# Softmax preparation moved into the second recurrent step and the second graph layer, layernorms placed afresh

## What is computed

```python
# L0: y = (adj @ x + x) @ weight + bias, each row divided by its length
# L1: 5 recurrent steps, in_matrix and out_matrix both adj
m = adj @ h
z = sigmoid([m, m] @ w3.T + b3 + h @ u3.T + ub3)
r = sigmoid([m, m] @ w4.T + b4 + h @ u3.T + ub3)
hv = tanh([m, m] @ w5.T + b5 + (r * h) @ u5.T + ub5)
h = (1 - z) * h + z * hv
# L2: A = adj + I, d = rowsum(A) ** -0.5
y = (d[:, None] * A * d[None, :]) @ x @ W.T + b
# L3: the k-th positive cell of adj gets e[k], cells that aren't positive get -9e15
A = softmax(where(adj > 0, e[cumsum(adj > 0) - 1], -9e15), axis=1)
y = (A * I) @ (x @ W[0]) + (A * (1 - I)) @ (x @ W[1]) + bias
```

## Time and profile before

| | us |
|---|---|
| median of 3 runs (lowest, highest) | 800.88 (800.42, 801.36) |
| the profiled execution's own time | 799.98 |
| its span, first to last instruction | 798.3 |
| PE busy | 770.0 (96%) |
| DVE busy | 651.3 (82%) |
| ACT busy | 515.2 (65%) |
| POOL busy | 117.1 (15%) |
| mean granted PE clock | 0.993 |

### The profile page before, as it was taken

The page is one execution under the profiler, slowest core; times in us unless marked ns, Lnnn a source line. Parts: engine busy times, 40 slices in busy tenths (PEclk is TensorE's granted clock), DMA queues, the critical chain, the costliest instruction groups (busy, mean ns, idle before and its releaser), DMA issues.

```text
span 798.3 us, 12062 instructions
## 1 busy us (share of the span) xinstructions
PE 770.0 (96%) x3822; PEld 638.7 (80%) x3824; DVE 651.3 (82%) x1578; ACT 515.2 (65%) x1050; POOL 117.1 (15%) x127
## 2 busy tenths in 40 slices
PE   7999988899999999999999999999999999999996
PEld 6888766687888888888888888888877787888885
DVE  6788999988877777777778777777999999986444
ACT  4768756678666666666666666666677766665445
POOL 1354422200000000000000000000112133332222
PEclk9999999999999999999999999999999999999998
DMA  6300000100100000000000000000000000000112
GB/s 186 128 1 2 1 0 1 53 1 9 45 1 0 1 1 0 0 0 0 0 0 0 0 0 0 0 1 1 1 1 1 1 2 1 1 0 14 53 54 93
DMA packets 8782, 13.09 MB, mean 16 GB/s; under 512 B 2336, under 2 KB 3872, under 8 KB 8480
## 3 DMA queue, kind: packets, MB, share of 16 engines
q1 hardware_dynamic: 8736, 12.53, 4.6%
HBM read 7.28 MB, written 5.24 MB: 16 GB/s over the span
## 4 chain that ended last, share of the span: by engine, by line
PE 67%; DVE 24%; ACT 5%; issue 2%; DMA 1%; SPq 0%; POOL 0%; ACTq 0%
PE agg_ps L930 11%; PE agg_ps L932 11%; PE agg_ps L931 11%; PE gate_ps L860 5%; PE gate_ps L862 5%; PE gate_ps L861 5%; PE cand_ps L860 3%; PE cand_ps L862 3%; DVE stats L765 3%; PE cand_ps L861 3%; PE turn_ps L969 3%; PE gate_ps L867 3%; PE cand_ps L867 3%; DVE nat_lo L777 2%; DVE cand L733 2%
## 5 line engine op out<-in xcount | busy, mean ns | idle before, releaser
L576 POOL TENSOR_TENSOR rstd<-mean_var,half 128x4 f32<-128x4 f32 x64 | 78.5, 1226 | 570.6 <-DVE mean_var L772 570.5
L930 PE MATMUL agg_ps<-adj_hi,nat_hi 128*128 128x512 f32 x384 | 151.9, 396 | 0.0
L932 PE MATMUL agg_ps<-adj_hi,nat_lo 128*128 128x512 f32 x384 | 150.1, 391 | 0.0
L931 PE MATMUL agg_ps<-adj_lo,nat_hi 128*128 128x512 f32 x384 | 149.6, 390 | 0.0
L462 ACT ACTIVATE reset_hi<-gate_r 128x512 fp32r<-128x512 f32 x80 | 50.6, 632 | 105.2 <-DVE gate_r L741 105.2
L724 DVE TENSOR_TENSOR agg_lo<-agg_ps,agg_hi 128x512 fp32r<-128x512 f32 x80 | 55.1, 689 | 63.6 <-ACT agg_hi L429 63.5
L390 ACT ACTIVATE res<-res,shift,rstd 128x128 f32<-128x128 f32 x210 | 87.9, 484 | 10.1 <-DVE shift L784 10.1
L932 PEld LDWEIGHTS agg_ps<-adj_hi,nat_lo 128*128 128x128 f32 x384 | 72.0, 188 | 16.1
L931 PEld LDWEIGHTS agg_ps<-adj_lo,nat_hi 128*128 128x128 f32 x384 | 72.2, 188 | 15.6
L930 PEld LDWEIGHTS agg_ps<-adj_hi,nat_hi 128*128 128x128 f32 x384 | 72.2, 188 | 15.0
L446 ACT ACTIVATE gate_r<-gate_ps,bias 128x512 f32<-128x512 f32 x80 | 55.1, 689 | 39.4 <-PE gate_ps L862 39.4
(11 more groups left out here) (174 smaller groups left out, 1705.6 us busy)
## 6 DMA issues: line engine op xcount, KB each, us to landing
res<-in_x SPq DMA_DIRECT2D x16, 256.0 KB, 5.5
out<-res SPq DMA_DIRECT2D x16, 256.0 KB, 2.0
rows<-in_adj SPq DMA_DIRECT2D x4, 256.0 KB, 3.9
mix_rows<-feat SPq DMA_DIRECT2D x1, 1024.0 KB, 3.9
later<-mix_rows SPq DMA_DIRECT2D x1, 1024.0 KB, 4.8
gate_z<-in_L_gnn_w_w SPq DMA_DIRECT2D x3, 128.0 KB, 5.4
gate_r<-in_L_gnn_bias SPq DMA_DIRECT2D x2, 64.0 KB, 5.5
gate_z<-in_L_gnn_u_w SPq DMA_DIRECT2D x2, 64.0 KB, 4.6
```

What stands on the lines that cost most here:

```text
L576: pool.tensor_tensor(rstd[:, i % RING, :], mean_var[:, i % RING, :, 1], half[:, :], ALU.pow).then_inc(rstd_made, 1)
L930: pe.matmul(ps, nat_hi[:, b, k, :], m_hi[:, k, :], start=(k == 0), stop=False)
L931: pe.matmul(ps, nat_hi[:, b, k, :], m_lo[:, k, :], start=False, stop=False)
L932: last = pe.matmul(ps, nat_lo[:, b, k, :], m_hi[:, k, :], start=False, stop=(k == T - 1))
```

## The change

The L0 layernorm moves up: added in slot n+4, measured in n+4, normed in n+6, split and turned in n+7, copied in n+8. Results of the fifth step are turned 4 to 10 slots after their unit, five in about seven slots; the transposes of L2 ("cross") come six slots later than before, in slots 107 to 122. Except in L0 and for the last unit, ACT norms all four quarters. Epsilon, the sign and the shift go from DVE to POOL, which has four operations a unit for its one. "chosen" and "value" go to slots 24 to 35, one every three slots; "late" comes in slots 26 to 35; exponentials to slots 99 to 102, scaling (now ACT, two a slot) to 104 and 105, diagonal to 105, "mix" turns to 106 to 109. `mix` and `chosen` now lie over eye_hi and eye_lo, `count` and `mask` over `later`. The raw scores, not the weights, go through DRAM. The L2 matrix no longer comes from POOL's sums: the adjacency is loaded a second time after slot 35, ACT scales its rows in slots 38 and 39, PE turns it in slots 41 to 44 and adds the diagonal by a small matmul. The loop covers two steps; step two is written out. W_L3 and W_SELF are loaded after the mix is stored. A Sigmoid stands at ACT's start.

```diff
-LOOP_FROM = 2 * B
-LOOPS = STEPS - 2
+LOOP_FROM = 3 * B
+LOOPS = STEPS - 3
...
-LAGS = {"turn": (0, 0), "add": (1, 1), "stats": (6, 1), "shift": (7, 2), "norm": (11, 3), "split": (12, 4),
-        "back": (13, 5)}
-RING = 16
-SLOTS = UNITS + 1 + LAGS["norm"][1] + 1
+LAGS = {"turn": (0, 0, 0, 0), "add": (2, 1, 1, 1), "stats": (2, 1, 1, 1), "norm": (4, 3, 3, 3), "split": (5, 4, 4, None),
+        "cross": (5, None, 10, None), "back": (6, None, 11, None)}
+RING = 8
+SLOTS = UNITS + 1 + LAGS["norm"][3] + 1
...
+    if is_inner(u):
+        return STATE_LAG
+    return 2 if stage(u) == L0 else STATE_LAG + (u - LAST) * 2 // 5 if is_step(u) else 1
+
+
+def lag(what, u):
+
+    if what == "add" and B - 2 <= u < B:
+        return 1
+    return LAGS[what][0 if stage(u) == L0 else 1 if is_step(u) else stage(u) - L2 + 2]
...
-    return [u for u in NORMED if u + turn_lag(u) + LAGS[what][stage(u) != L0] == s]
+    return [u for u in NORMED if lag(what, u) is not None and u + turn_lag(u) + lag(what, u) == s]
 
 
 def shared(n):
 
-    return stage(n) == L0 or n == UNITS - 1 or len(norms_at(n + turn_lag(n) + LAGS["norm"][1], "norm")) == 2
+    return stage(n) == L0 or n == UNITS - 1
...
 OWNER_AT = 3
-CHOSEN_AT = 5
-VALUE_AT = 9
+SUM_AT = 3
 WEIGHTS_AT = 13
-D_ROW_AT = B + 3
-
-SUM_AT = 3
-LATE_AT = 4
-EXP_AT = VALUE_AT + 1
-EYE_AT = B
-L2_ROWS_AT = D_ROW_AT + 1
-MIX_MADE_AT = B + 4
-L2_AT = L2_ROWS_AT + 6
-MIX_AT = AFTER + 9
-DIAGONAL_AT = AFTER + 4
+
+CHOSEN_AT = [B + 8 + 3 * k for k in range(T)]
+LATE_AT = [at + 2 for at in CHOSEN_AT]
+VALUE_AT = [at + 2 for at in CHOSEN_AT]
+SCALE_AT = VALUE_AT[-1] + 3
+L2_AT = SCALE_AT + 3
+assert L2_AT + T < LOOP_FROM
+
+EXP_AT = AFTER + 3
+INV_AT = EXP_AT + T
+WEIGH_AT = INV_AT + 1
+DIAGONAL_AT = INV_AT + 2
...
     if MIX_AT <= s < MIX_AT + T:
         found.append(("mix", s - MIX_AT))
-    found += [("back", u) for u in norms_at(s, "split") if stage(u) in (L0, L2)]
+    found += [("back", u) for u in norms_at(s, "cross")]
...
-    if VALUE_AT <= s < VALUE_AT + T:
-        found.append(("value", s - VALUE_AT))
-    if s == D_ROW_AT:
-        found.append(("d_row", 0))
+    if s in CHOSEN_AT:
+        found.append(("chosen", CHOSEN_AT.index(s)))
+    if s in VALUE_AT:
+        found.append(("value", VALUE_AT.index(s)))
+    if L2_AT <= s < L2_AT + T:
+        found.append(("l2", s - L2_AT))
...
         adj_lo = sb("adj_lo", [P, T, N], F32R)
+        with nc.sbuf_tensor("mix", [P, T, N], F32) as mix:
+            pass
         eye_hi = sb("eye_hi", [P, T, N], F32R)
+        with nc.sbuf_tensor("chosen", [P, T, N], F32) as chosen:
+            pass
         eye_lo = sb("eye_lo", [P, T, N], F32R)
         later = sb("later", [P, T, N])
...
-            sp.dma_start(mix_dram.rearrange("(p t) m -> p t m", t=T), mix).then_inc(mix_stored, 16)
+            sp.wait_ge(late_added, T)
+            sp.dma_start(later[:, :, :], adj.rearrange("(p t) m -> p t m", t=T)).then_inc(rows_again, 16)
+            sp.wait_ge(max_made, T)
+            sp.dma_start(mix_dram.rearrange("(p t) m -> p t m", t=T), mix[:, :, :]).then_inc(mix_stored, 16)
+            sp.dma_start(w_all[:, W_SELF, :], wl3[0]).then_inc(last_in, 16)
+            sp.dma_start(w_all[:, W_L3, :], wl3[1]).then_inc(last_in, 16)
             sp.wait_ge(mix_stored, 16)
-            sp.wait_ge(l2_lo_made, T)
+            sp.wait_ge(turn_read, reads(TURN_NO["l2", T - 1]))
             sp.dma_start(later[:, :, :], mix_dram.rearrange("(p t) m -> p t m", t=T)).then_inc(mix_loaded, 16)
             sp.dma_start(diag[:, :], mix_dram.rearrange("n m -> (n m)")[0:N * N:N + 1]
                          .rearrange("(p t) -> p t", t=T), allow_slow_non_contiguous=True).then_inc(diag_in, 16)
...
                         act.wait_ge(turned, k + 1)
-                        if n in (4, 6, 8, 10, 12):
-                            act.wait_ge(turned, TURN_NO["chosen", T - 1] + 1)
-                        if n == 6:
-                            act.wait_ge(late_added, T)
-                        if n == 8:
-                            act.wait_ge(turned, TURN_NO["value", T - 1] + 1)
-                        if n == 10:
-                            act.wait_ge(l2_made, T)
-                        if n == 12:
...
                         act.wait_ge(gate_done, n + 1)
                         for t in range(T):
-                            if n or t:
-                                act.wait_ge(squared, T * n + t)
-                            act.activation(square_out, layer_ps[n % 4][:, t * D:(t + 1) * D], ACT.Square,
...
                         act.wait_ge(row_sum_made, k)
-                    act.activation(feat[:, 3, :], rows[:, k, :], ACT.Copy, accum_out=row_sum[:, k:k + 1]).then_inc(row_sum_made, 1)
-                if s == 1:
+                    act.activation(feat[:, 15, :], rows[:, k, :], ACT.Copy, accum_out=row_sum[:, k:k + 1]).then_inc(row_sum_made, 1)
+                if s in CHOSEN_AT:
+                    k = CHOSEN_AT.index(s)
                     act.wait_ge(mask_made, T)
-                    act.wait_ge(const_made, consts)
-                    act.activation(flat(mix), mask, ACT.Identity, scale=-NEG, bias=neg[:, 0:1]).then_inc(neg_made, 1)
+                    act.activation(mix[:, k, :], mask[:, k * N:(k + 1) * N], ACT.Identity, scale=-NEG,
+                                   bias=neg[:, 0:1]).then_inc(neg_made, 1)
...
                                    ACT.Copy).then_inc(w_hi_made, 1)
+                for k in range(2 * (s - SCALE_AT), 2 * (s - SCALE_AT) + 2):
+                    if 0 <= k < T:
+                        act.wait_ge(rows_again, 16)
+                        act.wait_ge(row_d_made, 1)
+                        act.activation(later[:, k, :], later[:, k, :], ACT.Copy,
+                                       scale=row_d[:, k:k + 1]).then_inc(rows_scaled, 1)
+                k = s - L2_AT
+                if 0 <= k < T:
+                    act.wait_ge(mix_stored, 16)
+                    n = TURN_NO["l2", k]
+                    act.wait_ge(turned, n + 1)
+                    act.activation(eye_hi[:, k, :], turn_ps[n % 2][:, :], ACT.Copy,
+                                   scale=row_d[:, k:k + 1]).then_inc(l2_hi_made, 1)
                 k = s - EXP_AT
                 if 0 <= k < T:
-                    act.wait_ge(max_made, k + 1)
-                    act.activation(mix[:, k, :], mix[:, k, :], ACT.Exp, bias=row_max[:, k:k + 1],
+                    act.wait_ge(mix_loaded, 16)
+                    act.activation(later[:, k, :], later[:, k, :], ACT.Exp, bias=row_max[:, k:k + 1],
                                    accum_out=exp_sum[:, k:k + 1]).then_inc(exp_made, 1)
-                if s == EXP_AT + T:
-
-                    act.activation(e_last[:, :], neg[:, :], ACT.Sigmoid)
-                k = s - L2_AT
-                if 0 <= k < T:
-                    act.wait_ge(agg_done, B)
-                    act.wait_ge(l2_made, k + 1)
-                    act.activation(eye_hi[:, k, :], later[:, k, :], ACT.Copy,
-                                   scale=row_d[:, k:k + 1]).then_inc(l2_hi_made, 1)
+                    act.wait_ge(diag_in, 16)
+                    act.activation(diag[:, k:k + 1], diag[:, k:k + 1], ACT.Exp,
+                                   bias=row_max[:, k:k + 1]).then_inc(diag_exp_made, 1)
+                for k in range(2 * (s - WEIGH_AT), 2 * (s - WEIGH_AT) + 2):
+                    if 0 <= k < T:
+                        act.wait_ge(exp_inv_made, 1)
+                        act.wait_ge(diag_apart, k + 1)
+                        act.activation(later[:, k, :], later[:, k, :], ACT.Copy,
+                                       scale=exp_inv[:, k:k + 1]).then_inc(mix_made, 1)
                 k = s - MIX_AT
...
                     i = NORMED.index(n)
-                    pool.wait_ge(stats_made, i + 1)
-                    pool.tensor_tensor(rstd[:, i % RING, :], mean_var[:, i % RING, :, 1], half[:, :],
-                                       ALU.pow).then_inc(rstd_made, 1)
-                k = s - L2_ROWS_AT
-                if 0 <= k < T:
-                    pool.wait_ge(turn_read, reads(TURN_NO["d_row", 0]))
-                    pool.tensor_tensor(later[:, k, :], later[:, k, :], d_row, ALU.mult).then_inc(l2_made, 1)
-                k = s - EYE_AT
-                if 0 <= k < T:
-                    pool.wait_ge(eye_lo_made, T)
-                    pool.tensor_tensor(later[:, k, :], eye_hi[:, k, :].bitcast(F32), eye_lo[:, k, :].bitcast(F32),
-                                       ALU.add).then_inc(eye_made, 1)
+                    pool.wait_ge(aggregated, i + 1)
+                    r = mean_var[:, i % RING, :, 1]
+                    back = shift[:, i % RING, :]
+                    link(pool.tensor_scalar(back, mean_var[:, i % RING, :, 0], -1.0, None, ALU.mult))
+                    link(pool.tensor_scalar(r, r, EPS_LN, None, ALU.add))
```

(63 more changed lines are left out.)

76 lines of the change are left out of this document (33 added, 43 removed).

## The result

The changed kernel takes **781.41 us** (median of 4 runs, 781.29 to 781.96), the kernel before in the same rounds 800.65 (4 runs, 800.22 to 801.36): a ratio of 0.976, 95% interval 0.9743 to 0.9777. The gain is 19.2 us where 12.8 were forecast; the time lies 6.7 under the forecast and 1.1 under the lower end of the range. The profiled execution took 781.29, its span is 779.6 (before 798.3).

A forecast was written before the change was run, and what follows sets the result against it. TensorE was busy 96% of the span, with VectorE's lateness in the first recurrent step the one large reserve. Terms summed to -12.8 from 799.98, 787.2; the median, 0.9 higher, gave 788.1 us, range 782.5 to 797.

The forecast's parts named there:

- the one large reserve: First recurrent step, slots 16 to 31: takes 126.9 us against 105.6 of TensorE's work, VectorE being late; 21 us.
- The terms of TensorE's own work, in L0, the second step and L3: First layer -1.2 us, second step +4.5, third layer +2.7, from products and turns removed, added or moved.
- Rival A: GpSimd's four operations a unit block VectorE's low halves and norm by 1.0 us; end about 814 us; chance 0.06.
- VectorE: 4.7, 7.0, 8.1, 7.05 for slots 16 to 19: First half of first step: VectorE's work per slot in us, part of a 55.0 sum for slots 16 to 23, -9.0.
- I give back 0.8 for latency: Slots 24 to 31: 0.8 us added to the -7.7, since VectorE's slack shrinks from 1.4 to 0.5.
- L2, "+0.4": Second graph layer, then 77.8 us: turns moved out and in, plus 2.5 for ScalarE's excess; +0.4, bounds -2 and +5.
- the diagonal's 1.7: Second graph layer: TensorE's 1.7 us wait for the diagonal stays, its steps being still one slot apart.
- Rival B: ScalarE bounds: first layer at 4.8 a slot (+4.5), L2 with all 5 us and diagonal later (+4.5); 797; chance 0.16.
- The fifth step: Slots 84 to 95: results turned five in seven slots, 79.8 us against 39.6 + 43.9; -3.6.
- Three lost turns: Fifth step: of slots 84 to 95 three lose a turn of results, -1.4 us.
- VectorE's 7.1 us: Fifth step: VectorE holds 7.1 us of work in only four slots, +0.5 each, +2.0 in all.
- Rival C: All frictions vanish: fifth step at TensorE's rate (-2), L2 without ScalarE's excess (-2.5), 0.8 not needed; 782.8; chance 0.13.

The follow-up runs named there:

- the small products: The kernel before, with GpSimd's eight 128x512 operations of the L2 matrix cut to four columns and the scaled matrix left out of the output: 792.89 us.
- The two runs with more VectorE work: The changed kernel with one more 128x512 VectorE sum at the end of each of slots 16 to 19, or of 21 to 24: 784.11 and 781.52 us.
- the second of the runs with more work: The changed kernel with one more 128x512 VectorE sum at the end of each of slots 21 to 24: 781.52 us.

## Why the prediction was right, and where it failed

**Right.** The bound: VectorE in the first step, the one large reserve, which gave 19.5 of the 21 us. Its two parts were right too: GpSimd's plain products stretched VectorE's norm (7.8 us by the small products), and the L0 layernorms and the softmax pieces that stood in the stage were the rest. The terms of TensorE's own work, in L0, the second step and L3, held to 0.2 us, those for the second step and L3 being costs. L0's slots are 4.33 in the changed kernel: 4.22 for ScalarE against 4.31 was enough room. Rival A fell: no chain of GpSimd held VectorE up by the price of a product.

**The step that failed most:** "VectorE: 4.7, 7.0, 8.1, 7.05 for slots 16 to 19". VectorE's own work was that, but I took for each slot the longer of two engines, 26.85 in sum. Measured were 24.1, all but 0.07 of it TensorE's own work. What couples the engines is not the end of a turn but single results in it, above all reset_lo, which TensorE needs only after the next slot's aggregation. So VectorE could end a slot's work 4.5 us after TensorE had begun the next; it entered the stage with 0.1 of that used (78.66 against 78.54). Four slots over the bound, between stages that are under it, cost less than their sum: here 2.7 less. The two runs with more VectorE work show both sides of this, full price where the stock is used (slots 17 to 21) and none where it refills. That this stock explains the 2.7 is worked out from the timeline; a run that starts the stage with the stock already spent was not made.

**"I give back 0.8 for latency":** this term was not needed, 55.15 against 55.2 without it. Slack of 0.5 a slot on VectorE was enough, and the second of the runs with more work put 0.7 more into slot 24 and lengthened nothing.

**L2, "+0.4", measured -2.1.** TensorE's busy time there went from 75.27 to 73.60, -1.7 where I had -1.3. The rest is waits: 2.6 before, 2.2 after, and I had taken off 0.7, put on 2.5 for ScalarE and left the diagonal's 1.7, which makes 4.4. Measured: ScalarE's lateness cost 1.1 and 0.6, not 2.5 (it was busy for 65.3 us, not 71), and the diagonal's wait was 0.4. Leaving it at 1.7 was the wrong step: its length hangs on how late VectorE is, and the change took work off VectorE in this very stage, 73.2 to 66.4 us busy. Rival B's "diagonal later" had the sign wrong in the same way.

**The fifth step** came out right (-3.8 for -3.6) by two terms that were not. Three lost turns were to save 1.4; the slots without a turn (87, 90, 94) took 6.52, only 0.1 less than the others. Without the turn the z product stands behind ScalarE's reading of the gate bank: in slot 90 that ended at 579.20 (L450, from 578.51) and the product began at 579.26, 0.49 after the one ahead of it where 0.23 is usual. And VectorE's 7.1 us showed in one slot (95, 7.28), not in four, +0.7 instead of +2.0, presumably because it may run behind here too, which no run tested. That the errors cancel is luck. (As written, 79.8 against 83.5 is -3.7, and L2's terms add to +0.5.)

**Rival C** gave nearly the time (782.8), by a partly different way, which is luck: the 0.8 came, and L2's 2.5 in size, though ScalarE's waits were there; the 2 us in the fifth step did not (slots 90 to 95 at 6.7 on average, VectorE 37.5 busy of 40.1), and 2.7 came from slots 16 to 19, which no case had.

**The change as a whole.** Neither move pays alone: with small GpSimd products the kernel is at 792.9, with the norms early as well at 793.4, with the softmax moved but the norms late at 798.2, with both moved at 781.4. VectorE's L0 stage has room for one of the two, and the banks of the first step for the other only when the L0 turns are gone.

## What to carry to other kernels

Price a stretch of few overfull slots as a sum over the stretch with the stock of delay that the second engine may use, not slot by slot; price a long one slot by slot. The room in that stock is set by the one result that the other engine needs first, so look up when it is ready and when it is used. A wait for a busy engine grows and shrinks with that engine's load, so price each again when work moves onto or off it; and where two engines are near the bound, relieve both, since each alone leaves the other's wait (1.0 and 1.5 us singly, 3.9 together). Before moving work on an engine that two stages share, look at what else leaves or enters both stages and at how many buffers the moved results share.
